# Expert down products turned round: weights held, 512 tokens moved, sums kept with channels in partitions

## The reference, cut to what matters

```
p   = softmax(x2 @ w_router) * softmax((x2 @ w_gating) / 0.1)      # per token, over 8 experts
cw  = p / (sum_e p + 1e-9)                                          # (tokens, 8)
out = sum_e cw[:, e] * ((silu(x2 @ w_gate[e]) * (x2 @ w_up[e])) @ w_down[e])   # 256 -> 1024 -> 256
result = layernorm(x2 + out)                                        # over the 256 channels
```

## Time and profile before

| what | value |
|---|---|
| median of 3 runs | 1837.73 us (1837.53 to 1839.55) |
| the profiled execution | 1839.56 us, of which the span in the trace is 1837.8 us |
| TensorE busy (matmul) | 94% of the span, 10508 matmuls |
| VectorE busy | 68% of the span, but 4 to 5 tenths in the expert part |
| ScalarE busy | 53% of the span, 2 to 3 tenths in the expert part |
| mean granted TensorE clock | 0.983 of full speed |
| expert part | begins at about 871 us, its first down product at 916.8 us |

### The profile page before, as it was taken

The page is one execution under the profiler, slowest core; times in us unless marked ns, Lnnn a source line. Parts: engine busy times, 40 slices in busy tenths (PEclk is TensorE's granted clock), DMA queues, the critical chain, the costliest instruction groups (busy, mean ns, idle before and its releaser), DMA issues.

```text
span 1837.8 us, 27207 instructions
## 1 busy us (share of the span) xinstructions
PE 1733.5 (94%) x10508; PEld 1519.3 (83%) x10508; DVE 1242.9 (68%) x1910; ACT 972.6 (53%) x1499; POOL 3.6 (0%) x26
## 2 busy tenths in 40 slices
PE   3599999999999998998999999999999999999997
PEld 1378888877888787888899889998999989999896
DVE  7999999999999865888554445454454544445446
ACT  4688898888889773444533333333333332333323
POOL 0000000000000000000000000000000000000000
PEclk9799999999999998999999999999999999999999
DMA  4000010001000002111111011100101001020001
GB/s 143 1 26 16 12 47 18 7 7 63 1 12 29 1 30 89 44 55 45 55 35 35 1 35 35 34 32 3 34 34 34 11 23 34 34 74 0 1 1 41
DMA packets 34702, 56.59 MB, mean 31 GB/s; under 512 B 3030, under 2 KB 20412, under 8 KB 33596
## 3 DMA queue, kind: packets, MB, share of 16 engines
q1 hardware_dynamic: 34620, 55.47, 9.3%
HBM read 51.79 MB, written 3.67 MB: 30 GB/s over the span
## 4 chain that ended last, share of the span: by engine, by line
PE 80%; DVE 15%; ACT 2%; issue 2%; DMA 0%; SPq 0%; ACTq 0%; DVEq 0%
PE fbank L1900 33%; PE fbank L1922 17%; PE pair L804 7%; PE pair L792 6%; PE pair L769 6%; PE pair L779 4%; PE proj L1394 2%; DVE st L263 1%; PE pair L759 1%; DVE kfl L416 1%; PE qbanks L1430 1%; PE abanks L1430 1%; DVE aa L365 1%; DVE bb L361 1%; DVE pp L347 1%
## 5 line engine op out<-in xcount | busy, mean ns | idle before, releaser
L1722 DVE TENSOR_TENSOR hf<-sil,fbank 128x512 f32<-128x512 f32 (+1 forms) x256 | 158.9, 621 | 479.4 <-PE fbank L1900 407.8
L1827 ACT ACTIVATE sil<-fbank 128x512 f32<-128x512 f32 (+1 forms) x256 | 139.3, 544 | 615.0 <-PE fbank L1900 614.9
L1900 PE MATMUL fbank<-xh,wh 128*128 128x512 f32 (+1 forms) x1024 | 289.9, 364 | 1.2 <-ACT sil L1827 1.2
L1900 PE MATMUL fbank<-xh,wl 128*128 128x512 f32 (+1 forms) x1024 | 288.9, 363 | 0.0
L1900 PE MATMUL fbank<-xl,wh 128*128 128x512 f32 (+1 forms) x1024 | 288.7, 363 | 0.0
L1922 PE MATMUL fbank<-wl,hh 128*128 128x256 f32 x896 | 250.3, 279 | 0.0
L1922 PE MATMUL fbank<-wh,hh 128*128 128x256 f32 x896 | 250.2, 279 | 0.0
L1922 PE MATMUL fbank<-wh,hl 128*128 128x256 f32 x896 | 250.1, 279 | 0.0
L1900 PEld LDWEIGHTS fbank<-xl,wh 128*128 128x128 f32 x1024 | 184.4, 189 | 30.8
L1900 PEld LDWEIGHTS fbank<-xh,wl 128*128 128x128 f32 x1024 | 184.4, 189 | 30.3
L1900 PEld LDWEIGHTS fbank<-xh,wh 128*128 128x128 f32 x1024 | 180.7, 189 | 27.8 <-ACT sil L1827 1.6
(11 more groups left out here) (227 smaller groups left out, 3048.5 us busy)
## 6 DMA issues: line engine op xcount, KB each, us to landing
raw<-in_w_gate SPq DMA_DIRECT2D x16, 512.0 KB, 3.8
raw<-in_w_up SPq DMA_DIRECT2D x16, 512.0 KB, 4.7
raw<-in_w_down SPq DMA_DIRECT2D x16, 512.0 KB, 5.8
raw<-in_w_ck SPq DMA_DIRECT2D x4, 1024.0 KB, 4.8
raw<-in_w_cv SPq DMA_DIRECT2D x4, 1024.0 KB, 4.8
raw<-in_ctx_t SPq DMA_DIRECT2D x4, 750.0 KB, 6.1
ct<-in_ctx_t SPq DMA_DIRECT2D x4, 750.0 KB, 4.9
x<-in_x SPq DMA_DIRECT2D x4, 448.0 KB, 7.0
```

Source lines behind the costliest of these rows:

```text
L1722: dve.tensor_tensor(hf[i][:, 0:w], sil[i][:, 0:w], banks(e, t, f)[1][:, 0:w], ALU.mult).then_inc(hf_ready, 1)
L1827: act.activation(sil[f % 2][:, 0:w], banks(e, t, f)[0][:, 0:w], ACT.Silu).then_inc(sil_ready, 1)
L1900: ins = pe.matmul(banks(e, t, f)[k][:, 0:w], m[h][:, o:o + P], a[:, b, columns(c)], start=i == 0, stop=i == 3 * CB - 1)
```

## The change

What it does, in order:

- `down` holds 128x128 blocks of w_down and moves the tokens: for each of the two blocks of 128 output channels, 4 hidden blocks by 3 splits, 12 passes of as many columns as the group has (512 or 256). That is 24 passes for a full and 24 for the small group. The result has channels in partitions, two PSUM banks for a group, seen as one tensor of 1024 columns.
- `accumulate` is two VectorE instructions for a group: PSUM times `cwb` (the weight of each token, the same in all partitions) into `part_out`, and `part_out` added to `acc`. `acc` is now the memory of `x2t` (x2 with channels in partitions) and starts as x2, so that the sum at the end already holds it; the storing of x2, its load as `xk` and the add L1769 go away.
- `cwb`: in expert 0, TensorE turns `cw` (`turn_weights`, after `gate_up(0, 2, 0)`), VectorE copies it out (`keep_weights`, in round 2 at f = 1), SyncE stores it to memory (57 KB), and then loads each group's weights of one expert into all 128 partitions (four transfers per expert, 917 KB in all). In the loop SyncE issues the four for expert e after its two weight halves, each when `acc_done` says that the group's last use is over.
- At the end `turn_tokens(c)` turns `acc` back, 128x128 block by block, into the PSUM banks `pairs[c]`; `final_stats` reads it there (bn_stats from PSUM), and `final_norm` too, which writes to `normed`. On TensorE `turn_tokens(0)` stands before `down(7, 6)`, `turn_tokens(1)` before `down(7, 7)`, the other two behind it. On VectorE `final_stats(0)` moves from round 6 of expert 7 to behind the last `low_h`.

```diff
-            def accumulate(e, t, start):
...
-                    ps = bank[4 + 2 * (t % 2) + i // 2][:, (i % 2) * C:(i % 2 + 1) * C]
-                    own = e if t >= 0 else e - 1
-                    a, w = acc[:, k, :], cw[:, own, k:k + 1]
...
-                        ins = dve.scalar_tensor_tensor(a, ps, w, a, ALU.mult, ALU.add)
-                    ins.then_inc(acc_done, 1)
+            def accumulate(e, t):
+                c = t % GROUPS
+                w = columns(c).stop - columns(c).start
+                dve.wait_ge(down_done, e * DOWN_E + t + 1)
+                if 0 <= t < GROUPS:
+                    dve.wait_ge(cw_in[c], e * 16 + 32)
+                reached(dve, acc_done, e * ACC_E + t)
+                dve.tensor_tensor(part_out[:, :, 0:w], pairs[2 + t % 2][:, :, 0:w],
+                                  cwb[:, columns(c)].unsqueeze(1).broadcast_to([P, CB, w]), ALU.mult).then_inc(weighed, 1)
+                dve.wait_ge(weighed, e * ACC_E + t + 1)
+                dve.tensor_tensor(acc[:, :, columns(c)], acc[:, :, columns(c)], part_out[:, :, 0:w], ALU.add)\
+                    .then_inc(acc_done, 1)
...
             def down(e, t):
-                for i, k in enumerate(tiles(t % GROUPS)):
+                if is_first(e) and t == 1:
+                    pe.wait_ge(cwt_ready, 1)
+                for b in range(CB):
                     n = 0
...
                         for a, m in ((hh, wh), (hh, wl), (hl, wh)):
-                            ins = pe.matmul(bank[4 + 2 * (t % 2) + i // 2][:, (i % 2) * C:(i % 2 + 1) * C],
-                                            a[t % 2][:, f, i * P:(i + 1) * P],
-                                            m[h][:, DOWN + f * C:DOWN + (f + 1) * C], start=n == 0,
-                                            stop=n == 3 * FB - 1)
+                            o = DOWN + f * C + b * P
+                            ins = pe.matmul(pairs[2 + t % 2][:, b, 0:w], m[h][:, o:o + P], a[t % 2][:, f, 0:w],
+                                            start=n == 0, stop=n == 3 * FB - 1)
...
+            def turn_weights():
+                pe.wait_ge(cw_ready, 1)
+                pe.transpose(turned_cw, cw[:].rearrange("p e k -> p (e k)"), ident[:]).then_inc(cw_turned, 1)
+            def turn_tokens(c):
+                pe.wait_ge(acc_done, (E - 1) * ACC_E + GROUPS + c + 1)
+                if c < 2:
+                    pe.wait_ge(hf_ready, E * HID_E - 1 + c)
+                for k in tiles(c):
+                    for b in range(CB):
+                        ins = pe.transpose(tokens_out(c, k)[:, b * P:(b + 1) * P], acc[:, b, k * P:(k + 1) * P], ident[:])
+                ins.then_inc(out_turned, 1)
...
+            def load_weights(e, c):
+                sp.dma_start(cwb[:, columns(c)], io["cw"][:, columns(c)].rearrange("(o e) n -> o e n", o=1)[:, e, :]
+                             .broadcast_to([P, columns(c).stop - columns(c).start])).then_inc(cw_in[c], 16)
+            sp.wait_ge(cwt_ready, 1)
+            sp.dma_start(io["cw"].rearrange("e (k p) -> (e k) p", p=P), cwt[:]).then_inc(cw_kept, 16)
+            sp.wait_ge(cw_kept, 16)
+            for c in range(GROUPS):
+                load_weights(0, c)
             with sp.Fori(1, E) as e:
...
+                for c in range(GROUPS):
+                    sp.wait_ge(acc_done, e * ACC_E + c - GROUPS + 1)
+                    load_weights(e, c)
...
             def final_stats(c):
-                xc = xk[:, k.start:k.stop, :]
-                dve.wait_ge(xk_in, 16)
-                after(did(dve.tensor_tensor(xc, xc, acc[:, k.start:k.stop, :], ALU.add)))
+                dve.wait_ge(out_turned, c + 1)
                 for i in k:
-                    last = did(dve.bn_stats(st[:, i, :], xk[:, i, :]))
+                    last = did(dve.bn_stats(st[:, i, :], tokens_out(c, i)))
...
+                final_stats(0)
+                accumulate(E - 1, STEPS_E - 2)
+                final_scale(0)
                 final_stats(1)
-                accumulate(E - 1, STEPS_E - 2, False)
-                final_scale(0)
                 final_stats(2)
-                accumulate(E - 1, STEPS_E - 1, False)
+                accumulate(E - 1, STEPS_E - 1)
                 final_scale(1)
```

More of the change, by code:

```diff
@@ L151, in rwkv_phase @@
         params_in = sem("params_in")
-        x_in = [sem(f"x_in{c}") for c in range(GROUPS)]
+        x_in = g["group_in"] = [sem(f"group_in{c}") for c in range(GROUPS)]
         wexp_done, w_ready = sem("wexp_done"), sem("w_ready")
@@ L1009, in sync @@
                     load_x(c)
[L1010 to L1018, removed]
+            sp.wait_ge(ctl_ready, B - CG)
+            load_half(sp, g["raw"][1], io, 0, 1, g["raw_in"][1])
         def vector(dve):
@@ L1561, in sem @@
             return ctx.enter_context(nc.semaphore(name))
-        x, ident, raw, raw_in, x2_kept = g["x"], g["ident"], g["raw"], g["raw_in"], g["x2_kept"]
+        ident, raw, raw_in = g["ident"], g["raw"], g["raw_in"]
         eps = sb("eps4", [P, 1])
-        xh, xl, xt, logit, acc = g["xh"], g["xl"], g["x2t"], g["logit"], g["acc"]
+        xh, xl, acc, logit = g["xh"], g["xl"], g["x2t"], g["logit"]
         top, total, rec = (sb(n, [P, 2 * TILES]) for n in ("ltop", "ltotal", "lrec"))
@@ L1575, in expert_phase @@
         hl = [sb(f"hl{i}", [P, FB, COLS], F32R) for i in range(2)]
-        xk = sb("xk", [P, TILES, C])
+        normed = sb("normed", [P, TILES, C])
         st, mv = sb("fst", [P, TILES, 6]), sb("fmv", [P, TILES, 2])
         lnv, y0, yy, rstd, shift = (sb(n, [P, TILES]) for n in ("flnv", "fy0", "fyy", "frstd", "fshift"))
-        bank = [tiles_.enter_context(nc.psum_tensor(f"fbank{i}", [P, 512], FP32)) for i in range(8)]
-        eps_set, xk_in = sem("feps_set"), sem("xk_in")
+        cwt, cwb, part_out = sb("cwt", [E * TILES, P]), sb("cwb", [P, N]), sb("part_out", [P, CB, COLS])
+        pairs = [tiles_.enter_context(nc.psum_tensor(f"fbanks{i}", [P, 2, COLS], FP32)) for i in range(4)]
+        bank = [pairs[i // 2][:, i % 2] for i in range(8)]
+        turned_cw = bank[6][0:E * TILES, 0:P]
+        eps_set = sem("feps_set")
+        cw_turned, cwt_ready, cw_kept = (sem(n) for n in ("cw_turned", "cwt_ready", "cw_kept"))
+        cw_in = g["group_in"]
+        weighed, out_turned = sem("weighed"), sem("out_turned")
         xl_ready, logit_ready = g["xl_ready"], g["logit_ready"]
@@ L1593, in expert_phase @@
         HID_E = STEPS_E * FB
-        DOWN_E = TILES
-        ACC_E = 2 * TILES
+        DOWN_E = ACC_E = STEPS_E
         SPLIT_E = 6
@@ L1604, in tiles, with tokens_out @@
             return range(c * COLS // P, min((c + 1) * COLS, N) // P)
[L1606 to L1612, removed]
+        def tokens_out(c, k):
+            i = k - tiles(c).start
+            return pairs[c][:, i // 2, (i % 2) * C:(i % 2 + 1) * C]
         def reached(engine, semaphore, count):
@@ L1711, in combine_weights, with keep_weights @@
                     .then_inc(cw_ready, 1)
-                dve.wait_ge(cw_ready, 1)
+            def keep_weights():
+                dve.wait_ge(cw_turned, 1)
+                dve.tensor_copy(cwt[:], turned_cw).then_inc(cwt_ready, 1)
             def times_up(e, t, f):
@@ L1757, in expert @@
                             low_weights(e_, h_, j)
+                        if is_first(e) and t == AHEAD and f == 1:
+                            keep_weights()
                         if f == FB - 1:
-                            accumulate(e, t - 2, is_first(e) and t - 2 < GROUPS)
-                    if isinstance(e, int) and e == E - 1 and t == STEPS_E - 2:
-                        final_stats(0)
+                            accumulate(e, t - 2)
             def final_stats(c):
                 k = tiles(c)
-                xc = xk[:, k.start:k.stop, :]
-                dve.wait_ge(xk_in, 16)
-                dve.wait_ge(acc_done, (E - 1) * ACC_E + accs(STEPS_E - GROUPS + c) + len(k))
-                after(did(dve.tensor_tensor(xc, xc, acc[:, k.start:k.stop, :], ALU.add)))
+                dve.wait_ge(out_turned, c + 1)
                 for i in k:
-                    last = did(dve.bn_stats(st[:, i, :], xk[:, i, :]))
+                    last = did(dve.bn_stats(st[:, i, :], tokens_out(c, i)))
                 after(last)
@@ L1816, in high_h @@
                 if f == 0:
-                    reached(act, down_done, e * DOWN_E + downs(t - 1))
+                    reached(act, down_done, e * DOWN_E + t - 1)
                 act.wait_ge(hf_ready, e * HID_E + n + 1)
@@ L1855, in final_norm @@
                 for k in tiles(c):
-                    ins = act.activation(acc[:, k, :], xk[:, k, :], ACT.Identity, bias=shift[:, k:k + 1],
+                    ins = act.activation(normed[:, k, :], tokens_out(c, k), ACT.Identity, bias=shift[:, k:k + 1],
                                          scale=rstd[:, k:k + 1])
@@ L1905, in down @@
             def down(e, t):
-                h = t // GROUPS % 2
```

(31 more changed lines are left out.)

19 lines of the change are left out of this document (4 added, 15 removed).

## The result

The changed kernel takes 1843.01 us (median of 20 runs, 1840.43 to 1844.33), the kernel before, beside it, 1838.75 (20 runs, 1836.33 to 1841.06). The ratio is 1.0018, 95% interval 1.0012 to 1.0025: about 3.3 us slower by the ratio, 4.3 by the medians, where the prediction had 3.4 us faster and a range up to 1837.8. The profiled execution of the changed kernel took 1843.53 us, its span 1841.8, so 4.0 us more span than before.

A forecast was written before the change was run, and what follows sets the result against it. Starts of TensorE's passes bound the kernel to the last gate block's end, then VectorE, ScalarE and the last store; -6.3 (down) + 0.15 (turn) + 2.8 (end) = -3.4 us, from 1837.73 to 1834.3 us, range 1829.0 to 1837.8.

The forecast's parts named there:

- I take gate's pace: Down blocks on TensorE: full 5.44 us against 5.60, small 2.88 against 2.80; 6.3 us saved over 62 blocks.
- The bounds: Down blocks' gain: at least 3.2 us at the RWKV passes' 15.3 ns, at most 11.3 at down's own 10.0 ns.
- The tail: From the last gate block's end to norm 1's start: 15.7 us against 12.9, so 2.8 us more.
- The turn of cw: On TensorE in expert 0: one pass and a change of form, 0.15 us.
- The round trip: cw stored and loaded before VectorE's first accumulate: 6 us taken, 7.9 allowed, 11.8 the upper bound; cost 0.
- The accumulates' cover: VectorE's 2.5 us per round hidden behind at least 5.6 us of TensorE work, in 64 rounds; cost 0.
- SyncE's queue: Weight halves wait behind four cwb loads, with above 40 us left for a load of under 7 us; cost 0.
- Stats 2: VectorE at the end: begins at 11.7 us, just after TensorE has group 2 turned at 11.2, so no wait.
- B: Rival: down passes keep their 10 ns beside the columns; -8.3 us, 1829.4 us; chance 0.18.
- C: Rival: moved tokens in down cost what L792's passes do; -0.2 us, 1837.5 us; chance 0.12.
- D: Rival: granted clock falls to 1.2 GHz behind down(7, 6), stats 2 starts 3.3 us later; 1837.6 us; chance 0.07.
- E: Rival: cw's way through memory holds VectorE and TensorE in expert 0; 5.4 us at upper bound, 1839.7 us; chance 0.07.

The follow-up runs named there:

- e1: The changed kernel without the unused 224 bytes (gap_h) in front of hh0; 1833.21 us in one run, against 1840.21 for the kernel before.
- e11: e1's kernel, timed in 10 runs: 1835.39 us against 1839.71 for the kernel before, ratio 0.9975.
- e2: The kernel before without the same unused 224 bytes in front of hh0; 1848.68 us against 1840.21, one run each.
- e6: The changed kernel with 32 unused bytes in front of hh0 in place of 224; 1842.43 us against 1839.57 for the kernel before, one run each.
- e8: The changed kernel with 224 unused bytes in front of weights wh0 and hh brought back to 128; 1854.29 us against 1839.57 for the kernel before, one run each.
- e9: The changed kernel with 224 unused bytes in front of wh0 and none in front of hh0; 1847.01 us in one run against 1839.71 for the kernel before.
- e4: The changed kernel with xh and xl moved in the down passes in place of hh and hl (output not the reference's); 1835.18 us in one run.
- e12: e11 with VectorE's and ScalarE's final stats, scales and norms in another order; 1834.71 us (6 runs), ratio 0.9967 to the kernel before.
- e5: The changed kernel with 288 unused bytes in front of hh0 in place of 224; 1843.20 us against 1839.57 for the kernel before, one run each.
- e7: The changed kernel with 128 unused bytes in front of hh0 in place of 224; 1842.53 us against 1839.57 for the kernel before, one run each.
- e3: The changed kernel with the splits as outer loop of a down block and the four hidden blocks as inner one; 1838.82 us in its run.

## Why the prediction was wrong

**The step that failed** is "I take gate's pace: a full block 24 x 226.8 ns = 5.44 us, against 5.60, saves 0.16". It measured 5.60: nothing saved in 47 blocks, 7.5 us of the sum gone. The rows it rested on agreed in form, clock and arrangement, but not in the place of the operands. With the place made equal (e1) the step comes out to the hundredth: 5.44 us, and 2.87 for a small block (2.88 predicted); an expert takes 115.28 us from down block to down block, 0.91 less than before, where 0.80 were forecast, and e11 is 4.6 us faster by the ratio, where the prediction had 3.4. The 224 bytes suited the old arrangement, which e2 shows: without them the old passes cost 119.8 ns in place of 116.7. The clue was in the code, an allocation that nothing reads, just in front of the tensors that change their part, and I passed over it. The sentence "holding the weights seems to cost a little per pass" falls with the step: tokens held cost 119.8 too when they lie where the weights do (e2), and weights held cost 116.8 at distance 32 (e6). Why the distance has this effect stays open.

**The bounds failed with it.** 3.2 to 11.3 us was to hold the gain of the down blocks before the last gate block's end; it was -0.4. The lower bound came from L792 at 202.0 ns for 448 columns; at 233.3/512 a column that is 204, at the pace of distance 0 (12.8 + 0.418 ns a column, from 119.8 and 226.8) it would be 200. By the allocation ckh is moved 192 bytes off its weights, so L792's 15.3 ns may well have been the same effect; that was not tried. As bounds I had treated three figures of "beside the columns" as costs of a pass. At distance 32, where the old passes stood, the cost goes with the columns (116.8 and 233.4 for 256 and 512 in e6); the new ones stand at 224, where 512 columns cost the same 233.3, and so halving the passes saved nothing.

**What held.** The tail: 15.70 us to norm 1 against 15.7 forecast, +2.74 against +2.8. That it fits to the hundredth is in part luck: down(7, 6), taken at 5.44, took 5.69 us and the two scales 0.25 more than their terms, and shorter accumulates and stats made up for it (2.40 and 1.30 us for 2.5 and 1.44, 3.47 for 3.64), as did a start 0.1 earlier. The turn of cw: from its start to the second pair of gate passes behind it are 0.57 us, where a pair takes 0.45, so 0.12 us against 0.15. The round trip: covered, 5.2 us against 6. The accumulates' cover and SyncE's queue: TensorE waits nowhere between the first down block and the end of the last gate block. Stats 2 did not wait for its turn. The small block, 2.83 against 2.88, was off the forecast on the good side: its distance is 224 and not 0.

**The rivals.** B (down keeps 10 ns a pass) and C (L792's remainder) both supposed a cost per pass. D did not happen: the granted clock is 1.00 in every 2 us from 1818 to 1830. The Trainium skill ("TensorE: Matmul & The Clock Gate", "Part 4: PE-mode transpose") says that turns do not engage the full clock. No run here shows it either way: 24 turns stand in this stretch, 16 of them between passes, and the clock stayed at 1.00. E did not happen. Its term of 1.5 us, for a low clock behind an idle TensorE, leaned on a row that doesn't show that the earlier trace rows: there the low clock came with TensorE in use all through, on 40 products of 16 columns and then eight turns. The result is on E's side, but not by its mechanism; what was missing was a rival in which the new passes cost just twice the old ones: by the sum 0.5 for the small blocks and 2.8 for the tail, 3.3 us slower, which is what the ratio gives (the traces have 0.42 + 2.74 - 0.38 = 2.8 without the scatter).
The Trainium skill's 2.5 ns beside the columns of a pass (same page, "Wait - 56ns, not 53.3ns?") is not what the float32r passes of the expert part show: the least there are 10.0 ns with 256 columns and 13.3 with 512.

## What to carry to other kernels

Before a row's pace is taken over for a changed operand, compare where the operands lie as well as their shapes; padding that nothing reads is a setting fitted to the present roles, and has to be fitted again when held and moved operands change places. Ask of a cost "beside the columns" whether it goes with the pass or with the column: two sizes at the same placement tell. And look at a change's tail as its own sum: here it cost 2.7 us to norm 1, well over a third of the 6.9 us that the well-placed passes give in the expert part (899.3 to 892.4).

## What the runs showed of the hardware

Pace of float32r passes with 128x128 held, TensorE busy all through at the granted clock 1.00, by the distance of the moved operand's place from the held one's, in bytes modulo 256 (each is a block's length, the median of all of its kind, divided by its passes):

| distance | 256 columns | 512 columns | seen in |
|---|---|---|---|
| 0 | 119.6 to 120.1 ns | 226.7 to 227.7 ns | gate in all runs but e8 and e9; down in e1, e2, e4, e9 to e12 |
| 32 | 116.6 to 116.8; 117.8 in e8's down | 233.3 to 233.5 | down before and in e5, e6, e8; gate in e8 and e9 |
| 128 | 119.8 | 233.0 | down in e7 |
| 224 | 118.3 | 233.4 | down in the changed kernel and e3 |

With 256 columns it was seen in both arrangements at distances 0 and 32, weights held or tokens held; with 512 columns only with weights held. Distances of 0 and 256 bytes do the same, 32 and 288 too. The best place for 256 columns is not the best for 512. Other distances, other widths of the held operand, and the cause were not tried.

A single profile can mislead by more than the effect: the first down block started between 913.34 us (e3) and 918.07 us (e11) in the fourteen profiles. Ahead of it TensorE does 40 products of 16 columns (from 900.98 us in e3, 902.47 in e11), turns eight blocks and does 24 gate passes, and by run the granted clock falls from the narrow products on or doesn't. Windows of e3 and then of e11 (PE busy, granted clock, DMA share, GB/s):

```profile
905.00:910.00 5.00, 5.00 (x30) 1.00 0.00 0
910.00:915.00 5.00, 5.00 (x31) 1.00 0.00 0
```
```profile
905.00:910.00 5.00, 5.00 (x28) 0.59 0.00 0
910.00:915.00 5.00, 5.00 (x17) 0.73 0.00 0
```

e3 keeps 2.4 GHz there; e11 falls to 1.2 GHz for part of it. The lengths of blocks, read inside one trace, don't show it, and the experiments are decided by them: most were run once, and a single time would not do.
